# Attention and FP4 feed-forward on one core: the second score pass moved ahead of the small TensorE jobs, the exponential ahead of its step's ScalarE jobs

## The chip, the core and the metric

The kernel runs on one core of a Trainium2 chip. TensorE multiplies, VectorE and ScalarE read its results out of PSUM, GpSimd works on data in SBUF, and SyncE issues the DMAs. Each engine takes its instructions in the order in which they are written and waits on semaphores. The metric is device microseconds for one execution; a row that carries "PE" is TensorE, "DVE" VectorE, "ACT" ScalarE, "POOL" GpSimd, "SP" SyncE.

## The reference

Input is x of shape 4 x 1024 x 128. One layer of attention with 16 heads over a latent of width 64, a layer norm, a feed-forward network whose operands are rounded to FP4 in blocks of 16, and another layer norm.

```python
k_eff = (W_dq.T @ W_uq.T @ W_uk).reshape(nh, hs, n_kvl)
v_eff = transpose((W_uv.T @ W_o.T).reshape(n_kvl, nh, hs), (1, 0, 2))
c_kv = x @ W_dkv.T
q = (x @ W_dq.T @ W_uq.T).reshape(B, T, nh, hs)
q_lat = einsum('bqhd,hdl->bhql', q, k_eff)
attn = softmax(where(causal, einsum('bhql,bkl->bhqk', q_lat, c_kv) / sqrt(hs), -inf))
y = einsum('bhql,hld->bqhd', einsum('bhqk,bkl->bhql', attn, c_kv), v_eff)
x = layernorm(x + y)
gate, up = fp4(x) @ fp4(w_gate).T, fp4(x) @ fp4(w_up).T
x = layernorm(x + fp4(silu(gate) * up) @ fp4(w_down).T)
```

## The kernel before

A batch of 1024 rows is attended in four quads of four heads. A quad is 18 **steps**, so a batch has 72; steps are numbered n = 0 to 71 in a batch, and s = n mod 18 in a quad. The scores are computed twice. The **first pass** (`score_max`, lines 520 and 507) makes rows of scores only so that VectorE can take their row maxima (line 837, `maximum`). The maxima are split in three bf16 parts on GpSimd (`top_split`), transposed (job `mt`), copied by ScalarE (line 686) and written by six small DMAs as extra rows of the query operand. The **second pass** (`score_probs`, lines 537 and 507) then makes transposed scores with the maximum already subtracted, and ScalarE takes their exponential (line 715, `exps`). The **weighing** (`weigh`, line 556) multiplies the values by them into `yt_ps`; it has twelve parts a quad, at steps s = 3, 5, 6, 7, 9, 10, 12, 14, 16, 17 and, in the next quad, 0 and 1. The first pass runs 24 steps ahead of the second.

Both passes write to one ring of three PSUM tiles of two banks. At step n the first pass may start when the exponential of step n-2 has been read out of its tile, and the second pass when the maximum of the first pass of step n-1 has. So the order in the ring is first pass, second pass, first pass, and so on.

Everything else that TensorE does is a **job** (`misc_job`), and nearly all jobs use one PSUM bank, `misc`: a job waits until the reader of the job before has emptied it (`frees`). A table (`jobs`) gives the step of each. `xt`, `k`, `q`, `v` prepare the next batch (steps 6, 7, 12, 15, 18, 19, 24, 25); `yn` (s = 3 and 9) normalizes the attention's output; `mt` (s = 13) is told above; `x1t`, `gate`, `up`, `ht`, `down` are the feed-forward network of the batch before, in eight tiles, `gate` at n = 4 + 6t, `up` at 5 + 6t, `ht` at 20 + 6t, `down` at 42, 43, 64 and 65. ScalarE reads `xt`, `k`, `q`, `v`, `mt`, `x1t`, `gate` and `ht` (`misc_read`); VectorE reads `yn` and `up` and adds `down`, and it makes the rest of `q`. Two steps after `gate` ScalarE also does `sigmoid` (lines 722 and 724), which waits for GpSimd's clamp (line 1151) of what the exponential of `gate` wrote.

The order of each engine is written out by a loop over batches and steps; there is no scheduler. In one step TensorE does: first pass, jobs, second pass, weighing. ScalarE does: reads of the jobs, `first_k_part` (steps 16, 17), `sigmoid`, exponential, copy of `yt_ps`. VectorE does: maximum, then its part of the jobs, then stages of the norms and of the quantization. SyncE's list after step 24 is long: when the last part of `q` is made it issues 24 copies to scratch in DRAM, then four reads, then the six rows of maxima for the quad that starts at step 36. A last loop (b = B) has only the feed-forward network of the last batch.

Of the kernel before, what the change touches and what calls it, by code (L numbers as in the profile page):

```python
# [49 lines left out]
def build(nc, x, w_dq, w_uq, w_dkv, w_uk, w_uv, w_o, w_gate, w_up, w_down, out):  # L50
    B, T, C = x.shape
# [78 lines left out]
    def jobs_at(b, n):  # L130
        return [(kind, b + d, k) for s, kind, d, k in (jobs if b < B else tail) if s == n and 0 <= b + d < B]
# [16 lines left out]
    with ExitStack() as ctx:  # L148
# [171 lines left out]
        def tile_pos(b, a, s):  # L320

            u = a + s // STEPS
            return b + u // QUADS, u % QUADS, s % STEPS
# [93 lines left out]
        def _(pe):  # L417
# [174 lines left out]
            for b in range(B + 1):  # L592
                if b == B:

                    pe.wait_ge(t_exp.sem, t_exp.at(B - 1, BODY - 1))
                for n in range(BODY):
                    if b < B:
                        a, s = n // STEPS, n % STEPS
                        nb, na, ns = tile_pos(b, a, s + STEPS + LEAD)
                        if nb < B:  # L600
                            if n < 2 and b == 0:
                                pe.wait_ge(s_max.sem, STEPS + LEAD)
                            else:
                                pn = b * BODY + n - 2
                                pe.wait_ge(t_exp.sem, pn + 1)
                            score_max(nb, na, ns, 2 * n % 3)
                    for job in jobs_at(b, n):
                        misc_job(*job)
                    if b < B:

                        if nb < B:
                            pe.wait_ge(s_max.sem, b * BODY + n + STEPS + LEAD)
                        else:
                            pe.wait_ge(s_max.sem, B * BODY)
                            pe.wait_ge(t_exp.sem, b * BODY + n - 2)
                        score_probs(b, a, s, (2 * n + 1) % 3)

                    for w, at in enumerate(W_STEP):
                        g = n - at
                        if g % STEPS == 0 and g >= 0 and b < B:  # L620
                            weigh(b, g // STEPS, w)
                        elif g % STEPS == 0 and g < 0 and b > 0:
                            weigh(b - 1, QUADS - 1, w)
# [3 lines left out]
        def _(act):  # L627
# [23 lines left out]

            def misc_read(kind, b, k):
                _, to = bank(kind, b, k)
                if kind == "xt":
                    act.wait_ge(xt_mm.sem, xt_mm.at(b, k))
# [116 lines left out]
            for b in range(B + 1):  # L772
                for n in range(BODY):
                    a, s = n // STEPS, n % STEPS
                    for job in jobs_at(b, n):
                        misc_read(*job)
                    if n in K_PART_AT and b + 1 < B:
                        first_k_part(b + 1, K_PART_AT.index(n))
                    if b > 0:
                        for stage, t in tile_at(b, n, H_A if b < B else TAIL_H_A):  # L780
                            sigmoid(b - 1, t)
                    if b < B:
                        exps(b, a, s)

                    if s == 7 and b < B:
                        out_copy(b, NC * a)
                    if s == 1:
                        if a > 0 and b < B:
                            out_copy(b, NC * a - 1)
                        elif a == 0 and b > 0:  # L790
                            out_copy(b - 1, QUADS * NC - 1)
# [428 lines left out]
```

## Time and profile before

| | us |
|---|---|
| median of 3 runs | 754.0 |
| lowest and highest | 752.06, 757.2 |
| profiled execution, its own time | 758.44 |
| its span | 756.6 |

The span has a stretch of preparation up to the first exponential at 71.7 us, the four batches up to about 665 us, and the tail of the last feed-forward network. In the stretch from 371 to 533 us, which is about one batch, TensorE is busy 136.09 us of 162, VectorE 131.71, ScalarE 101.46, GpSimd 74.91, at a granted TensorE clock of 0.95. Where a view says "idle before" it is the time in which the engine stood still ahead of that group, and the arrow names what ended the wait. A wait for a semaphore shows only with the one that came last.

### The profile page before, as it was taken

The page shows a single profiled execution, that of the slowest core. Times are in us where ns is not written, and L with a number is a line of the kernel's source. Part 1 is how long each engine was busy: PE and PEld are TensorE (multiplying, and loading weights), DVE is VectorE, ACT ScalarE, POOL GpSimd, SP SyncE. Part 2 cuts the span into 40 slices and gives each one's busy share as a digit, 9 for nine tenths or more (in the row PEclk, how much of TensorE's full clock was granted, in tenths as well). Part 3 has the DMA queues.
Part 4 walks back from the last instruction along what each step waited for, and adds up shares of the span by engine and source line. Part 5 has one row for each costly group of instructions (what it writes and reads, how often), then busy time and mean ns, then how long its engine had stood idle before and what let it go on. Part 6 is the DMA issues. An engine that isn't in the chain of part 4 may idle for free.

```text
span 756.6 us, 15168 instructions
## 1 busy us (share of the span) xinstructions
PE 563.6 (74%) x5863; PEld 254.3 (34%) x5863; DVE 532.3 (70%) x981; ACT 412.3 (54%) x598; POOL 316.0 (42%) x441
## 2 busy tenths in 40 slices
PE   4275988589787888788888889696978897862623
PEld 2132333233333434333333334242323342421412
DVE  0389787388889767788788778888787784264461
ACT  2311766377665766565576666564656675742220
POOL 4520032000436654433337464533273536258682
PEclk9655999799998999999898999998899998995565
DMA  3393006602300192020300480203000000000000
GB/s 101 77 241 101 2 3 151 145 2 51 94 5 12 31 210 56 15 52 16 92 16 2 90 196 11 56 10 78 3 16 3 3 2 16 1 15 0 0 14 15
DMA packets 34222, 37.91 MB, mean 50 GB/s; under 512 B 6390, under 2 KB 19766, under 8 KB 34150
## 3 DMA queue, kind: packets, MB, share of 16 engines
q1 hardware_dynamic: 33238, 36.39, 20.0%
q8 instruction: 47, 0.77, 0.4%
q10 hardware_dynamic: 912, 0.54, 0.3%
q14 instruction: 25, 0.20, 0.1%
HBM read 19.64 MB, written 16.78 MB: 48 GB/s over the span
## 4 chain that ended last, share of the span: by engine, by line
PE 39%; DVE 31%; POOL 13%; issue 10%; ACT 4%; DMA 2%; SPq 1%; POOLq 0%; DVEq 0%; ACTq 0%
DVE top L837 19%; PE yt_ps L556 11%; PE ring L537 6%; PE ring L520 5%; PE misc L495 3%; PE ring L507 2%; PE misc L466 2%; POOL eg L1151 2%; POOL hx L1123 2%; POOL hx L1121 2%; POOL hx L1125 1%; DVE z L906 1%; PE misc L455 1%; PE misc L486 1%; DVE hc L963 1%
## 5 line engine op out<-in xcount | busy, mean ns | idle before, releaser
L837 DVE TENSOR_REDUCE top<-ring 128x2 f32<-128x1024 f32 (+3 forms) x384 | 349.6, 948 | 113.4 <-PE ring L507 80.2
L715 ACT ACTIVATE probs<-ring 128x1024 f32<-128x1024 f32 x288 | 293.8, 1027 | 132.1 <-PE ring L507 79.7
L556 PE MATMUL yt_ps<-probs,v_op 128*32 128x512 f32 (+3 forms) x1536 | 171.6, 520 | 0.5 <-ACT probs L715 0.5
L537 PE MATMUL ring<-q_op,k_op 59*128 59x512 bf16 (+3 forms) x768 | 124.0, 346 | 50.2 <-DVE top L837 40.3
L520 PE MATMUL ring<-k_op,q_op 56*128 56x512 f16 (+3 forms) x768 | 127.8, 355 | 44.5 <-ACT probs L715 18.9
L520 PEld LDWEIGHTS ring<-k_op,q_op 56*128 56x128 bf16 x768 | 38.4, 96 | 171.0 <-issue 116.8
L1144 POOL TENSOR_TENSOR r<-r,yq 128x128 f32<-128x128 f32 x32 | 14.6, 457 | 168.3 <-DVE yq L876 168.3
L537 PEld LDWEIGHTS ring<-q_op,k_op 59*128 59x128 f16 x768 | 37.7, 95 | 120.8 <-DVE top L837 58.7
L507 PE MATMUL ring<-ident,mask_s 64*128 64x64 bf16 x1024 | 59.5, 198 | 0.0
L507 PEld LDWEIGHTS ring<-ident,mask_s 64*128 64x128 bf16 x1024 | 47.7, 102 | 17.7 <-issue 5.0
L507 PEld LDWEIGHTS ring<-ident,mask_t 64*128 64x128 bf16 x1024 | 47.2, 100 | 18.2 <-issue 6.8
L507 PE MATMUL ring<-ident,mask_t 64*128 64x64 bf16 x1024 | 52.0, 196 | 0.0
L1151 POOL TENSOR_SCALAR eg<-eg 128x352 f32<-128x352 f32 x32 | 35.1, 1098 | 28.0 <-ACT eg L698 27.6
L722 ACT ACTIVATE eg<-eg,one 128x352 f32<-128x352 f32 x32 | 18.7, 586 | 41.0 <-POOL eg L1151 41.0
L556 PEld LDWEIGHTS yt_ps<-probs,v_op 128*32 128x32 f32 x1536 | 30.9, 110 | 29.6 <-issue 18.5
L1121 POOL TENSOR_TENSOR hx<-hx,hc 128x352 f32<-128x352 f32 x32 | 29.8, 931 | 20.7 <-DVE hc L966 20.7
L486 PE MATMUL ring<-ident,hx 128*128 128x128 f32 (+1 forms) x24 | 6.7, 414 | 42.6 <-POOL hx L1125 42.6
L1080 POOL TENSOR_SCALAR top_parts<-top_all 128x32 bf16<-128x32 f32 x16 | 4.8, 297 | 68.3 <-DVE top_all L846 68.2
L1123 POOL TENSOR_TENSOR hx<-hx,hc 128x352 f32<-128x352 f32 x32 | 29.8, 930 | 2.5
L1155 POOL TENSOR_TENSOR h<-gu,eg 128x352 f32<-128x352 f32 x32 | 29.8, 930 | 0.0
L963 DVE TENSOR_SCALAR hc<-hx 128x352 uint32<-128x352 uint32 x32 | 15.8, 492 | 16.3 <-POOL hx L1160 16.3
L1125 POOL TENSOR_TENSOR hx<-hx,h_sc 128x352 f32<-128x352 f32 x32 | 25.2, 787 | 2.5
(170 smaller groups left out, 758.4 us busy)
## 6 DMA issues: line engine op xcount, KB each, us to landing
q_op<-scratch_q SPq DMA_DIRECT2D x32, 224.0 KB
k_op<-scratch_k SPq DMA_DIRECT2D x32, 224.0 KB
scratch_k<-k_part SPq DMA_DIRECT2D x32, 192.0 KB, 3.3
scratch_q<-q_part SPq DMA_DIRECT2D x32, 128.0 KB, 3.1
scratch_q<-q_part SPq DMA_DIRECT2D x16, 192.0 KB, 3.3
xp<-in_L_attn_x_dram SPq DMA_DIRECT2D x4, 512.0 KB, 4.4
r<-in_L_attn_x_dram SPq DMA_DIRECT2D x8, 256.0 KB, 2.8
out_dram<-z SPq DMA_DIRECT2D x8, 256.0 KB, 2.3
```

Of the source, the lines that this page charges most:

```text
L507: last = nc.tensor.matmul(ring[slot][:, e, at + HALF * half:at + HALF * (half + 1)], mask[group, half, :], ident16[group, group], start=Fa ...
L520: last = nc.tensor.matmul(ring[slot][:, e, at:at + n], q_op[lo:lo + ROWS, pair, i * P:(i + 1) * P], k_op[lo:lo + ROWS, pair, kc * CHUNK:kc ...
L537: last = nc.tensor.matmul(ring[slot][:, e, at:at + n], k_op[lo:lo + rows, pair, j * P:(j + 1) * P], q_op[lo:lo + rows, pair, (c + 1) * CHU ...
L556: last = nc.tensor.matmul(yt_ps[32 * q:32 * (q + 1), lo:CHUNK], v_op[:, j, 4 * a + q, :], probs[:, (STEPS * a + tile) % P_RING, q % 2, at: ...
L715: nc.scalar.activation(probs[:, n % P_RING, :, :], ring[(2 * n + 1) % 3][:, :, :], ACT.Exp, scale=SCALE).then_inc(t_exp.sem, 1)
L837: last = nc.vector.tensor_reduce(top[:, kc, :, p, i], ring[slot][:, :, at:at + n], AX.X, ALU.max)
L963: nc.vector.tensor_scalar(hc[:, n, :, :].bitcast(U32), hx[:, n, :, :].bitcast(U32), 0x7F800000, None, ALU.bitwise_and).then_inc(he_v.sem, 1)
L1121: nc.gpsimd.tensor_tensor(dst, dst, magic, ALU.add).then_inc(s1.sem, 1)
L1123: nc.gpsimd.tensor_tensor(dst, dst, magic, ALU.subtract).then_inc(s2.sem, 1)
L1125: nc.gpsimd.tensor_tensor(dst, dst, sc_, ALU.mult).then_inc(s3.sem, 1)
L1151: nc.gpsimd.tensor_scalar(eg[:, n, :], eg[:, n, :], EXP_TOP, None, ALU.min).then_inc(e_p.sem, 1)
L1155: nc.gpsimd.tensor_tensor(hn.rearrange("p n k -> p (n k)"), gu[:, n, :], eg[:, n, :], ALU.mult).then_inc(h_p.sem, 1)
```

## The change

On TensorE the second score pass of a step directly follows the first, and the jobs come behind both, ahead of the weighing as before. On ScalarE the exponential of a step comes ahead of that step's job reads, `first_k_part` and `sigmoid`; the copy of `yt_ps` stays where it is. No instruction is added or taken away, and VectorE, GpSimd and SyncE keep their lists.

```diff
--- before.py
+++ after.py
@@ -604,8 +604,6 @@
                                 pn = b * BODY + n - 2
                                 pe.wait_ge(t_exp.sem, pn + 1)
                             score_max(nb, na, ns, 2 * n % 3)
-                    for job in jobs_at(b, n):
-                        misc_job(*job)
                     if b < B:
 
                         if nb < B:
@@ -614,7 +612,8 @@
                             pe.wait_ge(s_max.sem, B * BODY)
                             pe.wait_ge(t_exp.sem, b * BODY + n - 2)
                         score_probs(b, a, s, (2 * n + 1) % 3)
-
+                    for job in jobs_at(b, n):
+                        misc_job(*job)
                     for w, at in enumerate(W_STEP):
                         g = n - at
                         if g % STEPS == 0 and g >= 0 and b < B:
@@ -772,6 +771,8 @@
             for b in range(B + 1):
                 for n in range(BODY):
                     a, s = n // STEPS, n % STEPS
+                    if b < B:
+                        exps(b, a, s)
                     for job in jobs_at(b, n):
                         misc_read(*job)
                     if n in K_PART_AT and b + 1 < B:
@@ -779,9 +780,6 @@
                     if b > 0:
                         for stage, t in tile_at(b, n, H_A if b < B else TAIL_H_A):
                             sigmoid(b - 1, t)
-                    if b < B:
-                        exps(b, a, s)
-
                     if s == 7 and b < B:
                         out_copy(b, NC * a)
                     if s == 1:
```

TensorE, batch 1, steps 40 and 41 (`L520` and `L507` with mask_s the first pass, `L537` the second, `L480` the jobs `gate` and `up`, `L556` the weighing), before:

```order
L520 MATMUL ring<-k_op,q_op 128x256 [waits t_exp]
L520 MATMUL ring<-k_op,q_op 128x256
L507 MATMUL ring<-ident,mask_s 128x64 x4
L520 MATMUL ring<-k_op,q_op 128x256 x2
L507 MATMUL ring<-ident,mask_s 128x64 x4
L480 MATMUL misc<-wu_t,xq_t 128x352 [waits x1t_cp,g_cp]
L537 MATMUL ring<-q_op,k_op 128x512 [waits s_max]
L537 MATMUL ring<-q_op,k_op 128x512
L556 MATMUL yt_ps<-probs,v_op 32x384 [waits t_exp]
```

and now:

```order
L520 MATMUL ring<-k_op,q_op 128x256 [waits t_exp]
L520 MATMUL ring<-k_op,q_op 128x256
L507 MATMUL ring<-ident,mask_s 128x64 x4
L520 MATMUL ring<-k_op,q_op 128x256 x2
L507 MATMUL ring<-ident,mask_s 128x64 x4
L537 MATMUL ring<-q_op,k_op 128x512 [waits s_max]
L537 MATMUL ring<-q_op,k_op 128x512
L480 MATMUL misc<-wu_t,xq_t 128x352 [waits x1t_cp,g_cp]
L556 MATMUL yt_ps<-probs,v_op 32x384 [waits t_exp]
```

The job `up` stood between the two passes and now stands between the second pass and the weighing; its waits are the same.

ScalarE, batch 1, steps 29 to 31 (`L715` the exponential, `L722` and `L724` `sigmoid` of step 30, `L686` the read of the job `mt` of step 31), before:

```order
L699 COPY gs<-misc 128x352
L715 ACTIVATE probs<-ring 128x1024 [waits av_mm,t_mm] x2
L722 ACTIVATE eg<-eg,one 128x352 [waits h_clamp]
L724 ACTIVATE eg<-eg 128x352 [waits h_ln]
L715 ACTIVATE probs<-ring 128x1024 [waits av_mm,t_mm]
L686 COPY top_t<-misc 96x128 [waits mrow_in,mt_mm]
L715 ACTIVATE probs<-ring 128x1024 [waits av_mm,t_mm]
```

and now (line numbers are one less there):

```order
L714 ACTIVATE probs<-ring 128x1024 [waits av_mm,t_mm]
L697 ACTIVATE eg<-misc 128x352 [waits g_gu,h_h,g_mm]
L698 COPY gs<-misc 128x352
L714 ACTIVATE probs<-ring 128x1024 [waits av_mm,t_mm] x2
L721 ACTIVATE eg<-eg,one 128x352 [waits h_clamp]
L723 ACTIVATE eg<-eg 128x352 [waits h_ln]
L714 ACTIVATE probs<-ring 128x1024 [waits av_mm,t_mm]
L685 COPY top_t<-misc 96x128 [waits mrow_in,mt_mm]
```

The rows read alike in sequence, but each exponential between two jobs is now the one of the earlier job's own step: the one ahead of `gate`'s read is that of step 28, the two behind it are steps 29 and 30, so `sigmoid` stands behind the exponential of its step and no longer in front of it.

## Rows read from the trace of the kernel before

**Rows 1.** The page: span, busy time by engine, shares of the chain that ended last.

```profile
span 756.6 us, 15168 instructions
...
PE 563.6 (74%) x5863; PEld 254.3 (34%) x5863; DVE 532.3 (70%) x981; ACT 412.3 (54%) x598; POOL 316.0 (42%) x441
...
PE 39%; DVE 31%; POOL 13%; issue 10%; ACT 4%; DMA 2%; SPq 1%; POOLq 0%; DVEq 0%; ACTq 0%
```

**Rows 2.** Groups by line; columns: count, busy us, mean ns, idle before, its releasers.

```profile
L837 DVE TENSOR_REDUCE top<-ring 128x2 f32<-128x1024 f32 (+3 forms) x384 | 349.6, 948 | 113.4 <-PE ring L507 80.2 <-PE ring L520 31.7
L715 ACT ACTIVATE probs<-ring 128x1024 f32<-128x1024 f32 x288 | 293.8, 1027 | 132.1 <-PE ring L507 79.7 <-PE ring L537 49.7
...
L520 PE MATMUL ring<-k_op,q_op 56*128 56x512 f16 (+3 forms) x768 | 127.8, 355 | 44.5 <-ACT probs L715 18.9 <-DMA k_op<-scratch_k 17.9 <-DVE top L837 7.2
L537 PE MATMUL ring<-q_op,k_op 59*128 59x512 bf16 (+3 forms) x768 | 124.0, 346 | 50.2 <-DVE top L837 40.3 <-issue 9.3
...
L722 ACT ACTIVATE eg<-eg,one 128x352 f32<-128x352 f32 x32 | 18.7, 586 | 41.0 <-POOL eg L1151 41.0
```

**Rows 3.** The same view: ScalarE's two copies that empty `misc` after `ht`.

```profile
L704 ACT COPY h_t<-misc 128x256 f32<-128x256 f32 x24 | 9.2, 384 | 3.6 <-PE misc L486 3.6
...
L705 ACT COPY h_t<-misc 96x128 f32<-96x128 f32 x24 | 6.6, 275 | 0.0
```

**Rows 4.** Timeline (start, length, instruction, idle before), batch 0, step 12.

```profile
89.06 1.23 DVE L837 TENSOR_REDUCE top<-ring 128x2 f32<-128x1024 f32 x1 [0.31 <-PE ring L507]
...
89.45 1.12 PE L451 MATMUL misc<-x_t,bk 128*128 128x512 f32 x2
...
90.50 0.39 PE L537 MATMUL ring<-q_op,k_op 59*128 59x512 bf16 x2
```

**Rows 5.** Timeline, batch 1, steps 40 and 41.

```profile
294.80 0.86 PE L480 MATMUL misc<-wg_t,xq_t 128*128 128x352 f32 x2
294.91 1.29 DVE L837 TENSOR_REDUCE top<-ring 128x2 f32<-128x256 f32 x2 [0.76 <-PE ring L507]
...
295.59 0.28 PE L537 MATMUL ring<-q_op,k_op 59*128 59x256 bf16 x2
...
295.69 0.46 ACT L698 ACTIVATE eg<-misc 128x352 f32<-128x352 f32 x1 [1.20 <-PE misc L480]
...
296.05 0.45 ACT L699 COPY gs<-misc 128x352 f32<-128x352 f32 x1
...
296.55 0.86 PE L480 MATMUL misc<-wu_t,xq_t 128*128 128x352 f32 x2
...
297.66 0.85 PE L556 MATMUL yt_ps<-probs,v_op 128*32 128x384 f32 x8
```

**Rows 6.** Timeline, batch 1, steps 48 to 50.

```profile
315.37 1.09 POOL L1151 TENSOR_SCALAR eg<-eg 128x352 f32<-128x352 f32 x1
...
316.50 0.59 ACT L722 ACTIVATE eg<-eg,one 128x352 f32<-128x352 f32 x1 [3.10 <-POOL eg L1151]
...
317.52 1.01 ACT L715 ACTIVATE probs<-ring 128x1024 f32<-128x1024 f32 x1
...
318.44 0.79 POOL L1125 TENSOR_TENSOR hx<-hx,h_sc 128x352 f32<-128x352 f32 x1
...
318.58 0.28 PE L520 MATMUL ring<-k_op,q_op 56*128 56x256 f16 x2 [2.41 <-ACT probs L715]
```

**Rows 7.** Timeline of SyncE's DMA issues, batch 1.

```profile
261.31 1.26 SPq L353 DMA_DIRECT2D scratch_k<-k_part  x3
...
280.62 4.29 SPq L371 DMA_DIRECT2D q_op<-top_t  x6
```

**Rows 8.** Timeline of TensorE, batch 1, step 36.

```profile
287.25 0.39 PE L537 MATMUL ring<-q_op,k_op 59*128 59x512 bf16 x2 [2.64 <-DVE top L837]
```

**Rows 9.** Timeline, batch 1, step 24, the job `q`.

```profile
256.73 1.13 PE L451 MATMUL misc<-x_t,aq 128*128 128x512 f32 x2 [0.36 <-DVE gu L939]
...
257.89 0.69 ACT L672 ACTIVATE q_part<-misc,q_scale 128x512 bf16<-128x512 f32 x1 [1.57 <-PE misc L451]
```

## The prediction, made before the changed kernel ran

> **What bounds the kernel now.** I read the page first, then the groups by line, then timelines of single steps. The profiled execution took 758.44 us (span 756.6 [rows 1]); the median of three runs is 754.0, so the profile lies 4.4 us above it. Sums are made against 758.44 and then moved down by 4.4.
>
> The page gives no single bound. TensorE is busy 74% of the span, VectorE 70%, ScalarE 54%, and the chain that ended last alternates: TensorE 39%, VectorE 31%, waits that nothing explains 10% [rows 1]. The groups by line say how [rows 2]: VectorE stood idle 113.4 us ahead of the maxima, always for a first pass; ScalarE 132.1 us ahead of the exponentials, always for a second pass; TensorE 44.5 us ahead of the first pass and 50.2 us ahead of the second. Of the 44.5, 17.9 us are one DMA in the preparation and 18.9 us waits for an exponential. Of the 50.2, 40.3 us are waits for a maximum. So TensorE is the engine on which the others mostly wait, and what the change does to the time is read from TensorE's order: does it stand idle more or less.
>
> **What the second pass wins by going first.** It starts earlier by the length of the job, and so does the exponential. Who waits for an exponential? ScalarE itself was idle 132.1 us ahead of it, so ScalarE gains nothing. TensorE waited 18.9 us for one before a first pass. That is the whole prize, and its largest pieces have one cause. At step 48 [rows 6] ScalarE's `sigmoid` stands ahead of the exponential. It waits for GpSimd's clamp, which ends at 315.37 + 1.09 = 316.46; then come `sigmoid`'s two halves, then the exponential from 317.52 to 318.53, and the first pass of step 50 starts at 318.58 after 2.41 us of idle. Six waits of this kind are 2.41 us each, 14.5 of the 18.9. With the exponential in front, the first pass of step 50 needs not wait for the clamp. But the next thing is late already: the job `ht` of step 50 needs GpSimd's product, which ends at 318.44 + 0.79 = 319.23, and the weighing of step 50 stands behind `ht` in both kernels. So only what had stood behind the stall and now runs inside it is won, the second pass of step 50 with its handover and part of the wait behind `ht`: about 0.7 us of 2.41. Two of the six lie in a stretch that a DMA chain bounds (below) and win nothing. Four times 0.7 is 2.8; of the other 4.4 us I take half, since behind them VectorE is as late as ScalarE: **minus 5 us**.
>
> It also runs in front of jobs that themselves wait for `misc` to be emptied, so 0.32 us of each such wait is used. But where ScalarE is in the chain of such a job (`q`, then `v`), its read now comes later by as much. I take ten places where it isn't, at 0.15: **minus 1.5 us**.
>
> **What it costs: cover.** The second pass waits for the maximum of the first pass of the step before. Till now a job ran in that time. Once the trace shows it whole [rows 4]: the maximum ends at 89.06 + 1.23 = 90.29; the job `k` runs from 89.45 to 90.5; the second pass starts at 90.50, 0.2 after the maximum, with no idle ahead of it. Now TensorE stands idle from 89.45 to 90.5, runs the second pass, and then the job: the weighing behind comes 1.0 us later. This is the upper price. Where the maximum has ended before the first pass is out, the price is zero. In batch 0, with no feed-forward jobs to slow TensorE down, the maxima are late at nearly every step; there are eight such jobs outside the stretch of the DMA chain (`yn` at n = 9, 21, 39, 45, 57, 63; `k` at 12; `q` at 18). One at 1.0 and seven at 0.45, the middle: **plus 4 us**. In batches 1 to 3 TensorE arrives later at most steps; I allow one full and two half cases in three batches: **plus 2 us**.
>
> **What it costs: the one bank of the jobs.** ScalarE now reads a job behind its step's exponential, and the next job waits for that read. The pair `gate`, `up` at a step with no weighing between them [rows 5]. Before: `gate` at 294.80, read from 295.69 to 296.05 + 0.45 = 296.50, `up` at 296.55, so the bank is free just in time. Now: second pass at 294.80, `gate` at 295.15 (the pass keeps TensorE for about 0.35 of its 0.39 us [rows 4], an estimate), the exponential from 295.3 to 296.3 (1027 ns [rows 2]), the read to 297.2. TensorE has meanwhile done the first pass of step 41 (until 296.55), the second, which needs the maximum ended at 294.91 + 1.29 = 296.20, and stands at `up` from 296.9 to 297.25. The weighing then starts at 298.03 and not at 297.66: 0.37 us. Steps 4, 22 and 40 of three batches have no weighing: 9 x 0.4, **plus 3.6 us**. At the other `gate`s a weighing of about 1 us hides it.
>
> The pair `ht`, `yn` is of the same kind. A second pass at time 0, exponential from 0.4 to 1.45, two copies of 0.38 and 0.28 us [rows 3]: `misc` is free at 2.1. TensorE is at `yn` at about 1.7, after its own pass, `ht`, a first pass and a second that waits a little for its maximum (four groups of 0.35 to 0.5 us, an estimate from rows 4 and 5). 0.3 us at five pairs a batch, three batches: **plus 4.5 us**.
>
> **What it costs: the chain through SyncE.** The last part of `q` (job of step 24, 256.73 [rows 9]) is read by ScalarE at 257.89, worked on by VectorE and GpSimd, and SyncE starts its list at 261.31; the six rows of maxima are issued from 280.62 to 284.9 [rows 7], and the second pass of step 36 starts at 287.25 after 2.64 us of idle [rows 8]. The view names VectorE for it, but the rows land just then. So in batches 0 to 2 whatever steps 25 to 35 win or lose is swallowed, and the start of the list moves with the job of step 24. There the second pass now comes first (0.32 us), and the read waits for the exponential that the second pass started (0.4 + 1.02 against 0.32 + 1.13, even): 0.4 us in three batches, **plus 1.2 us**. SyncE's other transfers wait for nothing that moves by more than 1 us, and they have many us of slack.
>
> **Costed at nothing.** VectorE takes the product of `up` 0.3 us later at its source, hidden by the 1.23 us maximum ahead of it in VectorE's queue; gone, it would be 24 x 0.3 = 7 us, my bound for this. `sigmoid` comes one exponential (1.03 us) later, and ScalarE waited 41.0 us for the clamp ahead of it [rows 2], so it mostly takes the place of waiting; GpSimd's product of it is due three steps later. The tail has no exponential and no scores, and its order is the same.
>
> **Sum.** 4 + 2 + 3.6 + 4.5 + 1.2 - 5 - 1.5 = 8.8, so about 9 us slower: 767 for an execution like the profiled one, **763 us** against the median of 754. Bounds: every cover term at its upper end and no prize gives 8 + 4 + 3.6 + 7 + 1.2 + 7 = 31 slower; every cover term at zero and the prize whole gives 18.9 + 3 less, 22 faster. Each end needs all terms at once.
>
> **A rule of the notes against the row.** The Trainium skill, "Perfetto Trace Analysis", section Identifying the Most-Contended Engine, says that the engine of highest occupancy is the one to work on. By that rule this change, which takes no work from TensorE, would leave the time alone: 754. The trace shows three engines near each other and none near full [rows 1], and a second pass whose free cover order alone makes [rows 4]; so here I go by order. The rule's result is the second case below.
>
> **The rivals, with chances.**
> - *Forecast, slower by 8 to 18 us, 0.50.* As above.
> - *Nothing measurable, 0.35.* The waits are elastic: a TensorE that arrives later at one second pass finds its maximum ready at the next, as VectorE with 70% is nearly as full, and the stalls behind `sigmoid` [rows 6] and SyncE's chain [rows 7] swallow what the steps in front of them lost. For it: after each such stall the account begins at zero. Against it: VectorE was itself idle 113.4 us for TensorE, so a late first pass mostly costs. If half of the positive terms (15.3) is swallowed, it is 7.6 - 6.5, plus 1: 755 us.
> - *Faster, 0.12.* The exponential is the real clock of the ring: with it early, the six stalls of 2.41 us go whole, the small ones too (18.9), and the cover terms fall to half (8). 754 - 11 = 743. Its place is the first pass behind `sigmoid`; it decides if the first pass of step 50 lets VectorE and through it GpSimd run ahead far enough that `ht` is no longer late by the time TensorE is there, more than about 1.5 us won per stall. Against it: `ht`'s product comes out of GpSimd's own queue behind the clamp.
> - *Slower by over 20 us, 0.03.* More idle ahead of second passes takes TensorE's clock down to 1.2 GHz for the steps behind; a `k` of 1.12 us would be 2 us. The mean clock of 0.95 would show it. 780 us.
>
> A measurement of this kernel can tell about 1%, 7.5 us. Slower by more: 0.50 + 0.03, less 0.03 for the low edge of the forecast's case, 0.50. Within: 0.35 + 0.03 - 0.01 for the low edge of that case, 0.37. Faster: 0.12 + 0.01 = 0.13. The range reaches from 748, leaving out most of the faster case, to 776, leaving out the last one and the top of the forecast.
>
> **What would show it.** Right: TensorE's idle ahead of `L537` for a maximum up from 40.3 to 55 us or more; idle ahead of `up` and `yn` for ScalarE's copies, 5 to 9 us more; idle ahead of the first pass for an exponential down from 18.9 to under 8; ScalarE's wait for the clamp down from 41.0 by 10 or more; the second passes of step 36 in batches 0 to 2 still idle ahead. Wrong: if the wait for the exponential falls and VectorE's idle ahead of the maxima falls below 105 us, the ring gained and the faster case holds; if TensorE's idle sums move from one line to another and their total stays within 3 us, the second case holds.

## The result, and the profile after

The changed kernel takes 762.5 us, the median of 20 runs (756.9 to 766.9); the kernel before took 755.1 beside it (20 runs, 752.1 to 760.8). The ratio is 1.0084, with a 95% interval of 1.0059 to 1.0109: 7.3 us slower by the medians, 6.3 by the ratio (0.0084 x 755). The forecast was 763. Below, microseconds of an experiment are worked out from its ratio in the same way. Ratios and mean clocks leave out executions in a slower state of the chip, such as one of experiment 11 with 863.1 us at a mean granted clock of 0.557.

The page of the changed kernel, its rows for the span, the busy time of each engine and the chain that ended last:

```profile
span 756.9 us, 15168 instructions
...
PE 559.1 (74%) x5863; PEld 250.3 (33%) x5863; DVE 533.2 (70%) x981; ACT 411.7 (54%) x598; POOL 315.2 (42%) x441
...
PE 40%; DVE 29%; POOL 12%; issue 10%; ACT 6%; DMA 2%; SPq 1%; POOLq 0%; ACTq 0%; DVEq 0%
```

The span is that of before, 756.9 against 756.6 us [rows 1], though the medians lie 7.3 us apart. Each of the two traces is one execution, and they are unlike in their clock: the one of after (own time 758.84 us, 3.6 below its median) had a mean granted clock of 0.892, the one of before (758.44, 3.3 above its median) 0.876. At the higher clock TensorE was busy 4.5 us less with the same 5863 instructions. So the traces are read here for idle time and for what ended it. Added up over the timeline from the first exponential to the last, TensorE's idle is 100.7 us before and 105.5 after: 4.8 more.

Groups by line of the changed kernel (count, then busy time and mean ns, then the idle before them with what ended it):

```profile
L835 DVE TENSOR_REDUCE top<-ring 128x2 f32<-128x1024 f32 (+3 forms) x384 | 349.4, 948 | 103.6 <-PE ring L507 62.5 <-PE ring L520 39.5
...
L520 PE MATMUL ring<-k_op,q_op 56*128 56x512 f16 (+3 forms) x768 | 128.3, 357 | 25.4 <-DMA k_op<-scratch_k 17.1 <-DVE top L835 7.2 <-ACT probs L714 0.7
L537 PE MATMUL ring<-q_op,k_op 59*128 59x512 bf16 (+3 forms) x768 | 122.3, 341 | 75.1 <-DVE top L835 62.6 <-issue 10.5
...
L466 PE MATMUL misc<-ident,yt 128*128 128x128 f32 x128 | 21.4, 291 | 6.8 <-ACT h_t L704 6.2
L480 PE MATMUL misc<-wu_t,xq_t 128*128 128x352 f32 x48 | 20.6, 511 | 3.3 <-ACT gs L698 3.3
...
L721 ACT ACTIVATE eg<-eg,one 128x352 f32<-128x352 f32 x32 | 18.7, 586 | 33.6 <-POOL eg L1149 33.6
...
L486 PE MATMUL misc<-ident,hx 128*128 128x128 f32 (+1 forms) x72 | 13.7, 302 | 14.2 <-POOL hx L1123 14.1
...
L870 DVE RECIPROCAL inv<-misc 128x16 f32<-128x16 f32 x32 | 8.2, 257 | 22.4 <-PE misc L466 21.9
```

The same view of before, for four small groups that are not among the rows ahead of the prediction:

```profile
L466 PE MATMUL misc<-ident,yt 128*128 128x128 f32 x128 | 21.6, 293 | 4.8 <-ACT h_t L705 2.7 <-ACT yt L731 1.1
...
L480 PE MATMUL misc<-wu_t,xq_t 128*128 128x352 f32 x48 | 20.6, 511 | 0.9
...
L486 PE MATMUL misc<-ident,hx 128*128 128x128 f32 (+1 forms) x72 | 14.0, 307 | 4.6 <-POOL hx L1125 4.6
...
L872 DVE RECIPROCAL inv<-misc 128x16 f32<-128x16 f32 x32 | 8.0, 249 | 17.4 <-PE misc L466 17.4
```

Read in pairs. Ahead of the second pass (`L537`) TensorE's wait for a maximum rose from 40.3 to 62.6 us [rows 2]. Ahead of the first pass (`L520`) its wait for an exponential fell from 18.9 to 0.7. Ahead of `yn` (`L466`) and `up` the waits for ScalarE's copies rose from 2.7 to 6.2 and from nothing that is listed (0.9 in all) to 3.3. Ahead of `ht` (`L486`) the wait for GpSimd's product rose from 4.6 to 14.1. ScalarE waited less for the clamp (`L721`), 33.6 against 41.0, and VectorE less ahead of the maxima, 103.6 against 113.4 [rows 2]. But VectorE's wait for `yn` (`L870`, before `L872`) rose from 17.4 to 22.4: part of its idle only changed its place.

Timeline of the changed kernel (start, length, instruction, idle before), batch 0, step 12, against [rows 4]:

```profile
88.81 0.38 PE L520 MATMUL ring<-k_op,q_op 56*128 56x512 f16 x2
...
90.08 0.39 PE L537 MATMUL ring<-q_op,k_op 59*128 59x512 bf16 x2 [0.83 <-DVE top L835]
...
90.40 1.13 PE L451 MATMUL misc<-x_t,bk 128*128 128x512 f32 x2
...
91.46 1.07 PE L556 MATMUL yt_ps<-probs,v_op 128*32 128x512 f32 x8
```

The cover is gone, as predicted: TensorE is idle for 0.83 us where `k` had run, and `k` and the weighing (`L556`) come behind. From the start of the first pass to the weighing it is 91.46 - 88.81 = 2.65 us. Before it was 1.74, with the weighing at 90.82 in the same view: 0.91 more.

Timeline, batch 1, steps 40 and 41, the pair `gate` (first row) and `up` (last), against [rows 5]:

```profile
296.66 0.86 PE L480 MATMUL misc<-wg_t,xq_t 128*128 128x352 f32 x2
296.77 1.02 ACT L714 ACTIVATE probs<-ring 128x1024 f32<-128x1024 f32 x1 [1.61 <-PE ring L507]
...
298.04 0.46 ACT L698 COPY gs<-misc 128x352 f32<-128x352 f32 x1
...
298.55 0.86 PE L480 MATMUL misc<-wu_t,xq_t 128*128 128x352 f32 x2 [0.36 <-ACT gs L698]
```

The exponential (`L714`) runs ahead of the reads of `gate`, the second read ends at 298.50, and `up` stands idle until then: 0.36 us. The sum had 0.35.

Timeline, batch 1, steps 48 to 50, against [rows 6]:

```profile
316.46 1.09 POOL L1149 TENSOR_SCALAR eg<-eg 128x352 f32<-128x352 f32 x1
...
317.58 0.59 ACT L721 ACTIVATE eg<-eg,one 128x352 f32<-128x352 f32 x1 [1.60 <-POOL eg L1149]
...
319.53 0.79 POOL L1123 TENSOR_TENSOR hx<-hx,h_sc 128x352 f32<-128x352 f32 x1
...
320.46 0.52 PE L486 MATMUL misc<-ident,hx 128*128 128x128 f32 x3 [2.05 <-POOL hx L1123]
...
320.91 1.91 PE L556 MATMUL yt_ps<-probs,v_op 128*32 128x512 f32 x8
```

The clamp (`L1149`) still ends late, at 317.55, and `sigmoid` (`L721`) waits for it, but the first pass does not: its 2.41 us [rows 6] are gone. In its place `ht` of step 50 (`L486`) stands idle for 2.05 us, until GpSimd's product (`L1123`) ends at 320.32. The weighing behind it takes 1.91 us, where the same eight products take 1.07 in the timeline of step 12. The view by windows of the changed kernel shows the clock beside it (stretch, its length, busy time of TensorE's matmuls and weight loads, VectorE, ScalarE and GpSimd, then the granted clock):

```profile
320.90:322.80 1.90, 1.90 (x11) 0.23 (x12) 0.00 (x0) 0.53 (x2) 1.05 (x2) 0.52 0.04 7
```

The granted clock is 0.52, about the lower of TensorE's two levels (1.2 of 2.4 GHz), behind 2.05 us of standing still. The kernel before has the same: 1.93 us for the weighing of step 50, behind its 2.41 us.

### The profile page after: what moved, and what is told of

The parts are those of the page before. It is cut to its first block, busy times and chain, and to the rows that moved or that the text cites. A ratio compares the mean times of both kernels' runs of the same rounds, so it can differ in the third digit from the quotient of the medians.

```text
span 756.9 us, 15168 instructions
## 1 busy us (share of the span) xinstructions
PE 559.1 (74%) x5863; PEld 250.3 (33%) x5863; DVE 533.2 (70%) x981; ACT 411.7 (54%) x598; POOL 315.2 (42%) x441
## 3 DMA queue, kind: packets, MB, share of 16 engines
q1 hardware_dynamic: 33238, 36.39, 19.9%
## 4 chain that ended last, share of the span: by engine, by line
PE 40%; DVE 29%; POOL 12%; issue 10%; ACT 6%; DMA 2%; SPq 1%; POOLq 0%; ACTq 0%; DVEq 0%
DVE top L835 19%; PE yt_ps L556 13%; PE ring L520 5%; PE ring L537 5%; PE misc L495 3%; PE misc L466 2%; PE misc L480 2%; POOL eg L1149 2%; PE ring L507 2%; ACT probs L714 2%; POOL hx L1121 2%; POOL hx L1119 2%; POOL hx L1123 1%; DVE z L904 1%; PE misc L451 1%
## 5 line engine op out<-in xcount | busy, mean ns | idle before, releaser
L835 DVE TENSOR_REDUCE top<-ring 128x2 f32<-128x1024 f32 (+3 forms) x384 | 349.4, 948 | 103.6 <-PE ring L507 62.5
L714 ACT ACTIVATE probs<-ring 128x1024 f32<-128x1024 f32 x288 | 294.3, 1027 | 193.5 <-PE ring L507 123.5
L537 PE MATMUL ring<-q_op,k_op 59*128 59x512 bf16 (+3 forms) x768 | 122.3, 341 | 75.1 <-DVE top L835 62.6
L556 PE MATMUL yt_ps<-probs,v_op 128*32 128x512 f32 (+3 forms) x1536 | 172.9, 524 | 0.6 <-ACT probs L714 0.5
L520 PE MATMUL ring<-k_op,q_op 56*128 56x512 f16 (+3 forms) x768 | 128.3, 357 | 25.4 <-DMA k_op<-scratch_k 17.1
L520 PEld LDWEIGHTS ring<-k_op,q_op 56*128 56x128 bf16 x768 | 38.2, 96 | 165.1 <-issue 103.9
L537 PEld LDWEIGHTS ring<-q_op,k_op 59*128 59x128 f16 x768 | 37.8, 95 | 114.5 <-DVE top L835 90.4
L507 PE MATMUL ring<-ident,mask_s 64*128 64x64 bf16 x1024 | 58.8, 197 | 0.0
L507 PEld LDWEIGHTS ring<-ident,mask_t 64*128 64x128 bf16 x1024 | 47.2, 100 | 19.2 <-issue 6.2
L507 PEld LDWEIGHTS ring<-ident,mask_s 64*128 64x128 bf16 x1024 | 47.0, 100 | 15.7 <-issue 3.8
L507 PE MATMUL ring<-ident,mask_t 64*128 64x64 bf16 x1024 | 51.8, 196 | 0.0
L1149 POOL TENSOR_SCALAR eg<-eg 128x352 f32<-128x352 f32 x32 | 35.0, 1094 | 35.0 <-ACT eg L697 34.6
L556 PEld LDWEIGHTS yt_ps<-probs,v_op 128*32 128x32 f32 x1536 | 30.8, 110 | 47.1 <-issue 34.7
L486 PE MATMUL ring<-ident,hx 128*128 128x128 f32 (+1 forms) x24 | 6.7, 414 | 42.9 <-POOL hx L1123 42.9
L721 ACT ACTIVATE eg<-eg,one 128x352 f32<-128x352 f32 x32 | 18.7, 586 | 33.6 <-POOL eg L1149 33.6
L466 PE MATMUL misc<-ident,yt 128*128 128x128 f32 x128 | 21.4, 291 | 6.8 <-ACT h_t L704 6.2
```

What stands on the lines that cost most here:

```text
L466: last = nc.tensor.transpose(to[:, n * P:(n + 1) * P], yt[:, k % 2, n * P:(n + 1) * P], ident[:, :])
L507: last = nc.tensor.matmul(ring[slot][:, e, at + HALF * half:at + HALF * (half + 1)], mask[group, half, :], ident16[group, group], start=Fa ...
L520: last = nc.tensor.matmul(ring[slot][:, e, at:at + n], q_op[lo:lo + ROWS, pair, i * P:(i + 1) * P], k_op[lo:lo + ROWS, pair, kc * CHUNK:kc ...
L537: last = nc.tensor.matmul(ring[slot][:, e, at:at + n], k_op[lo:lo + rows, pair, j * P:(j + 1) * P], q_op[lo:lo + rows, pair, (c + 1) * CHU ...
L556: last = nc.tensor.matmul(yt_ps[32 * q:32 * (q + 1), lo:CHUNK], v_op[:, j, 4 * a + q, :], probs[:, (STEPS * a + tile) % P_RING, q % 2, at: ...
L714: nc.scalar.activation(probs[:, n % P_RING, :, :], ring[(2 * n + 1) % 3][:, :, :], ACT.Exp, scale=SCALE).then_inc(t_exp.sem, 1)
```

## The experiments

All are the kernel before with an edit, or the changed kernel with one; the ratio is always to the kernel before. In the diffs `first` is the condition for the new order in a step.

**1. TensorE's part alone, ScalarE's as before.**

```diff
-                    for job in jobs_at(b, n):
-                        misc_job(*job)
...
                         score_probs(b, a, s, (2 * n + 1) % 3)
+                    for job in jobs_at(b, n):
+                        misc_job(*job)
```

> Only TensorE's part of the change: the second score pass ahead of the jobs; ScalarE keeps the old order. Theory A (TensorE loses its cover: it stands idle for maxima where a job used to run): most of the loss of the whole change stays, +5 to +9 us (ratio 1.007 to 1.012), idle ahead of L537 for a maximum stays near 63 us. Rival B (the loss is that ScalarE reads the jobs later, so the bank misc comes free later): +0 to +2 us, since the reads again come first. Idle ahead of the first pass for an exponential comes back to 10 to 19 us in both.

760.0 us, ratio 1.0061 [1.0023, 1.0099]. Groups by line:

```profile
L520 PE MATMUL ring<-k_op,q_op 56*128 56x512 f16 (+3 forms) x768 | 127.1, 353 | 48.1 <-ACT probs L719 22.5 <-DMA k_op<-scratch_k 17.9 <-DVE top L847 7.2
L537 PE MATMUL ring<-q_op,k_op 59*128 59x512 bf16 (+3 forms) x768 | 121.3, 338 | 73.7 <-DVE top L847 62.4 <-issue 9.5
...
L466 PE MATMUL misc<-ident,yt 128*128 128x128 f32 x128 | 21.4, 291 | 1.2 <-ACT h_t L709 1.2
```

TensorE's part alone gives 4.6 us of loss, anywhere from 1.7 to 7.5 by the interval, and the whole of the wait for maxima (62.4 us against 62.6). With it the prize is not there: the first pass still waits 22.5 us for exponentials. The bank's price is there in small part: `yn` waits 1.2 us for ScalarE and `up` 2.1, in place of 6.2 and 3.3.

**2. ScalarE's part alone, TensorE's as before.**

```diff
+                    if b < B:
+                        exps(b, a, s)
                     for job in jobs_at(b, n):
                         misc_read(*job)
...
-                    if b < B:
-                        exps(b, a, s)
```

> Only ScalarE's part of the change: the exponential ahead of the reads, first_k_part and sigmoid; TensorE keeps the old order (jobs, then second pass). Theory A: the reads come a whole exponential later, and only then the next job can run, but second passes keep their cover: between -2 and +4 us. Rival B: +6 to +12 us, since here ScalarE must even wait for the second pass before it reads a job that was done ahead of it.

809.2 us, ratio 1.0713 [1.0662, 1.0763]: far beyond every theory. Two groups by line, and a timeline of batch 1, steps 15 and 16 (`L719` is the exponential here, `L669` ScalarE's read of a `k`, `L480` the job `gate`):

```profile
L466 PE MATMUL misc<-ident,yt 128*128 128x128 f32 x128 | 21.3, 291 | 29.0 <-ACT h_t L709 24.5 <-ACT yt L735 4.4
L480 PE MATMUL misc<-wu_t,xq_t 128*128 128x352 f32 x48 | 20.6, 511 | 20.2 <-ACT gs L703 20.2
```

```profile
242.46 1.02 ACT L719 ACTIVATE probs<-ring 128x1024 f32<-128x1024 f32 x1 [1.80 <-PE ring L507]
...
243.38 0.58 ACT L669 COPY kf<-misc 128x512 f32<-128x512 f32 x1
...
244.01 0.86 PE L480 MATMUL misc<-wg_t,xq_t 128*128 128x352 f32 x2 [1.38 <-ACT kf L669]
...
244.81 0.34 PE L537 MATMUL ring<-q_op,k_op 59*128 59x384 bf16 x2
...
245.36 1.02 ACT L719 ACTIVATE probs<-ring 128x1024 f32<-128x1024 f32 x1 [1.40 <-PE ring L507]
```

The order makes a ring of waits. The read of `k` stands behind the exponential of step 15 (242.46 to 243.48); `gate` waits 1.38 us for the read; in TensorE's old order the second pass stands behind `gate`, so it starts at 244.81; and the exponential of step 16, with ScalarE idle 1.40 us, waits for it. `yn` and `up` together wait 44.7 us for ScalarE (24.5 and 20.2). TensorE's idle is 142.7 us against 100.7. So the two halves of the change do not add: ScalarE's costs 54 us alone. Behind TensorE's new order, where a second pass no longer waits for what a job waits for, it costs 1.7 us (1.0084 - 1.0061), and the overlapping intervals do not tell that from zero.

**3. The whole change, but only at steps 0 to 23 of batches 1 to 3.** In the traces this stretch had looked quicker.

```diff
-                    first = True
+                    first = b > 0 and n < 24
```

> The whole change, but only at steps n < 24 of batches 1 to 3; the old order in batch 0 and from step 24 on. In the profile of the changed kernel the exponentials of steps 0 to 24 span 53.7, 54.4 and 48.0 us in batches 1 to 3 against 57.6, 59.2 and 51.8 before, and the steps from 24 on span 2 to 9 us more. Theory C (the change wins at the steps whose jobs wait for VectorE, and loses at the others): -6 to -12 us, ratio 0.984 to 0.992. Rival D (the steps after 24 only give back a lead that something else bounds, the chain through SyncE or GpSimd, whatever their order is): -3 to +2 us.

754.9 us, ratio 0.9994 [0.9962, 1.0025]. No gain. The stretch had been measured between starts of exponentials, and these now stand at another place of their step. From here on stretches go by the start of the weighing, which both orders have last.

**4. The old order, with `sigmoid` alone behind the exponential of its step.**

```diff
+                    if b < B:
+                        exps(b, a, s)
                     if b > 0:
                         for stage, t in tile_at(b, n, H_A if b < B else TAIL_H_A):
                             sigmoid(b - 1, t)
-                    if b < B:
-                        exps(b, a, s)
```

> TensorE in the old order; ScalarE in the old order but for sigmoid, which comes behind the exponential of its step (the reads of the jobs stay ahead of it). It takes away what I named as the cause of the six 2.41 us waits of the first pass for an exponential. Theory A: these go, what is won is what the job ht does not take back, -2 to -6 us (ratio 0.992 to 0.997). Rival: the clamp and the product of GpSimd bound these steps, 0 +- 1 us. Idle of the first pass for an exponential under 6 us in both.

755.2 us, ratio 1.0005 [0.9969, 1.0041]. Groups by line:

```profile
L520 PE MATMUL ring<-k_op,q_op 56*128 56x512 f16 (+3 forms) x768 | 128.7, 358 | 28.4 <-DMA k_op<-scratch_k 18.0 <-DVE top L847 7.0 <-ACT probs L719 2.7
...
L486 PE MATMUL misc<-ident,hx 128*128 128x128 f32 (+1 forms) x72 | 14.4, 313 | 17.5 <-POOL hx L1135 17.5
```

The wait for the exponential is gone, 2.7 us against 18.9. `ht` waits 17.5 us for GpSimd against 4.6. TensorE's idle fell by 2.8 us in all (97.9 against 100.7), and of the time nothing is seen: by the interval between 2.3 us won and 3.1 lost. In TensorE's old order the prize is worth nothing that the runs can tell: it is one wait in two places.

**5 and 6. The whole change in batch 0 alone, and in batches 1 to 3 alone.**

```diff
-                    first = True
+                    first = b == 0
```

and `b > 0` in the second.

> The whole change, but only in batch 0. Theory A (lost cover at steps whose maximum is late): by the start times of the weighings, batch 0 has 3 to 4 us more in the changed kernel and in the one with TensorE's part alone, at steps 3 to 18, 24 to 46 and 50 to 63, so +3 to +5 us here (ratio 1.004 to 1.007). Rival D (the whole is elastic: what batch 0 loses is got back later): 0 +- 1 us.

> The whole change, but only from batch 1 on (batch 0 in the old order). Theory A as predicted: the bank of the jobs and the chain through SyncE cost about 9 us, cover 2, against a prize of 6, so +3 to +5 us. Rival E (in batches 1 to 3 wins and losses cancel, and all the loss is batch 0's): -1 to +1.5 us.

Batch 0 alone 757.1 us, 1.0024 [0.9994, 1.0055]; the others alone 759.6, 1.0047 [1.0019, 1.0075]. That is +1.8 and +3.6 us, together 5.4 of the 6.3; only the second is clear of zero. The wait for maxima rose by 2.3 us in the first (42.6) and 19.9 in the second (60.2). Between the weighings of step 3 of batch 0 and step 0 of batch 1 the traces show 126.0 us before, 129.7 after and 131.2 in batch 0 alone, so the traces say about +4 or +5 where the runs say +1.8, with an interval from -0.5 to +4.2. Whether batch 0 costs 2 or 4 us stays open.

**7. The whole change, but ScalarE reads `gate` and `ht` ahead of the exponential as before.**

```diff
+                    early = lambda job: job[0] in ("gate", "ht")
+                    for job in jobs_at(b, n):
+                        if early(job):
+                            misc_read(*job)
                     if b < B:
                         exps(b, a, s)
                     for job in jobs_at(b, n):
-                        misc_read(*job)
+                        if not early(job):
+                            misc_read(*job)
```

> The whole change, but ScalarE reads the jobs gate and ht ahead of the exponential of their step again (the other reads, first_k_part and sigmoid stay behind it). It takes away what I priced as the one bank of the jobs, 8.1 us. Theory A: idle ahead of up and yn for ScalarE's copies falls from 9.5 to under 4 us and the time by 3 to 8 us against the changed kernel, 754 to 760 us. Rival F (that wait only takes the place of a wait for a maximum at the same step): idle ahead of the second passes grows by as much, time 760 to 763 us.

758.1 us, ratio 1.0029 [1.0001, 1.0057], against 1.0084 for the whole change: about 4 us won, and the two intervals stand apart, by a hair. Groups by line:

```profile
L537 PE MATMUL ring<-q_op,k_op 59*128 59x512 bf16 (+3 forms) x768 | 123.3, 343 | 76.1 <-DVE top L852 63.8 <-issue 10.6
...
L466 PE MATMUL misc<-ident,yt 128*128 128x128 f32 x128 | 21.7, 294 | 1.2 <-ACT h_t L709 1.2
...
L480 PE MATMUL misc<-wu_t,xq_t 128*128 128x352 f32 x48 | 20.6, 511 | 2.1 <-ACT gs L703 2.1
```

The two waits for ScalarE are down to 1.2 and 2.1 us, while the wait for a maximum is 63.8, 1.2 higher. So the bank's price was real, and was partly handed on. The same two waits stand in experiment 1. Between it and this one the exponential moves ahead of `sigmoid` and the other reads: the first pass waits 0.7 us for exponentials instead of 22.5, and the ratios, 1.0061 and 1.0029, lie 2.4 us apart with intervals that overlap.

**8. Experiment 4, and `ht` of tiles 2 and 5 (steps 32 and 50) one step later.**

```diff
-        jobs += [(4 + 6 * t, "gate", -1, t), (5 + 6 * t, "up", -1, t), (20 + 6 * t, "ht", -1, t)]
+        jobs += [(4 + 6 * t, "gate", -1, t), (5 + 6 * t, "up", -1, t), (20 + 6 * t + (t in (2, 5)), "ht", -1, t)]
```

> TensorE and ScalarE in the old order, sigmoid behind its exponential as in e4_sigmoid, and the job ht of tiles 2 and 5 (steps 32 and 50) one step later. In e4_sigmoid the waits for an exponential went from 19.1 to 2.8 us of idle and those of ht for GpSimd rose from 4.6 to 17.5, with no change in the time. If ht is what holds the steps then, idle ahead of ht falls under 8 us and the time by 3 to 8 us against the kernel before (ratio 0.990 to 0.996). Rival G (GpSimd's chain bounds the stretch whatever stands where): 0 +- 1.5 us, and the idle turns up ahead of another line.

747.6 us, ratio 0.9902 [0.9874, 0.9931]: quicker than both kernels. Groups by line, then the timeline of batch 1 from the second pass of step 50 on:

```profile
L520 PE MATMUL ring<-k_op,q_op 56*128 56x512 f16 (+3 forms) x768 | 126.5, 352 | 29.9 <-DMA k_op<-scratch_k 17.6 <-DVE top L847 7.2 <-ACT probs L719 4.8
L537 PE MATMUL ring<-q_op,k_op 59*128 59x512 bf16 (+3 forms) x768 | 121.4, 340 | 60.7 <-DVE top L847 43.1 <-issue 16.7
...
L486 PE MATMUL misc<-ident,hx 128*128 128x128 f32 (+1 forms) x72 | 14.0, 306 | 3.3 <-POOL hx L1135 3.3
```

```profile
314.95 0.39 PE L537 MATMUL ring<-q_op,k_op 59*128 59x512 bf16 x2 [0.36 <-DVE top L847]
...
315.33 1.07 PE L556 MATMUL yt_ps<-probs,v_op 128*32 128x512 f32 x8
...
316.82 0.39 PE L520 MATMUL ring<-k_op,q_op 56*128 56x512 f16 x2 [0.42 <-ACT probs L719]
...
317.46 0.52 PE L486 MATMUL misc<-ident,hx 128*128 128x128 f32 x3 [0.25 <-POOL hx L1135]
```

The first pass of step 51 waits 0.42 us and `ht`, now in the same step, 0.25. The weighing of step 50 takes 1.07 us. From the weighing of step 48 to that of step 50 it is 3.5 us, where it was 7.1 before, 6.1 in the changed kernel and 7.1 in experiment 4. That `ht` has left this stretch is not the reason: to the weighing of step 52 it is 7.1 us, against 11.1 before and 11.4 in experiment 4.

Part of the gain goes with TensorE's clock. The view by windows, the kernel before and then this one:

```profile
318.90:326.00 7.10, 6.06 (x63) 2.09 (x59) 4.17 (x6) 4.31 (x6) 1.96 (x3) 0.76 0.03 6
```

```profile
314.00:321.00 7.00, 5.97 (x91) 2.65 (x89) 5.59 (x10) 5.70 (x10) 4.79 (x6) 1.00 0.03 6
```

In about the same busy time (6.06 and 5.97 us) TensorE does 63 matmuls at a granted clock of 0.76, and 91 at 1.00. Either edit alone leaves a long stand here: 2.41 us ahead of the first pass in experiment 10, 2.86 ahead of `ht` in experiment 4, where the eight products behind it again take 1.93 us. From the first exponential to the last, the trace of experiment 8 is 13.1 us shorter than that of before: 4.7 of it is idle of TensorE (96.0), 8.4 is busy time with the same instructions. These are single executions, whose own times lie 12.5 us apart. How much of the 7.4 us that the ratio gives is idle and how much is clock, no run separates.

Not every place pays, either. The stall of step 32 lies ahead of SyncE's chain, which ends at step 36. In batches 1 and 2 the weighings of steps 30 and 34 came closer together (9.6 and 11.1 us, now 8.0 each), but those of steps 23 and 36 did not (32.4 and 31.6 us, now 31.9 and 32.0): the second pass of step 36 stands idle 3.7 and 3.8 us, before 2.6 and 0.3. In batch 3, which prepares no batch and has no such chain, steps 23 to 36 went from 29.3 to 26.2.

**9 and 10. The same edit of `ht` on the whole change, and on the kernel before with nothing else.** The diff is the one of experiment 8.

> The whole change, and ht of tiles 2 and 5 one step later (steps 33 and 51). Theory H (the change is a loss of cover and of the bank, and the wait of ht for GpSimd is a separate thing that both orders share): it wins as much on the changed kernel as e8_ht did on e4_sigmoid, 6 to 9 us, so 753 to 757 us, -0.4 to +0.3% against the kernel before. Rival: with the second pass first there is nothing left behind ht but the weighing, so less is won, 0 to 3 us, 759 to 762 us.

> The kernel before with ht of tiles 2 and 5 one step later and nothing else; sigmoid stays ahead of its exponential. Theory H (two waits stand in a row, for the exponential behind sigmoid and for ht behind GpSimd, and each alone hides the other): -1 to +1 us, and the first pass still waits 15 to 20 us for exponentials. Rival: ht was the whole of it, -5 to -8 us as in e8_ht.

On the whole change 752.0 us, 0.9950 [0.9914, 0.9985], 10 us under the changed kernel (1.0084 - 0.9950, times 755). Alone 757.3 us, 1.0001 [0.9962, 1.0041], with these groups by line:

```profile
L520 PE MATMUL ring<-k_op,q_op 56*128 56x512 f16 (+3 forms) x768 | 128.6, 357 | 45.1 <-ACT probs L719 19.1 <-DMA k_op<-scratch_k 18.2 <-DVE top L847 7.2
...
L486 PE MATMUL misc<-ident,hx 128*128 128x128 f32 (+1 forms) x72 | 15.6, 333 | 0.2 <-POOL hx L1135 0.2
```

The mirror of experiment 4: now `ht` waits 0.2 us and the first pass its old 19.1. Either edit alone gives nothing, 1.0005 and 1.0001; both give 0.9902. And 0.9950 against 0.9902 is the price of the rest of the changed order once this stall is gone: 3.6 us, by intervals that just overlap.

**11. Experiment 8, and on TensorE the second pass first at the steps of `k`, `q` and `v` in batches 1 to 3.**

```diff
-                    first = False
+                    first = b > 0 and any(j[0] in ("q", "k", "v") for j in jobs_at(b, n))
```

> e8_ht, and in batches 1 to 3 the second pass first at the steps whose jobs are k, q or v (12, 15, 18, 19, 24, 25). There the job itself waits for VectorE (7.7 + 2.7 us of idle in the kernel before). If the wait for the product of up and the wait for the maximum end one behind the other on VectorE, as in the changed kernel, the second pass only takes over the idle time: -1.5 to +1.5 us against e8_ht. If the order was what held it, -3 to -6 us against e8_ht.

749.2 us, ratio 0.9920 [0.9890, 0.9949], no better than 0.9902. Groups by line:

```profile
L537 PE MATMUL ring<-q_op,k_op 59*128 59x512 bf16 (+3 forms) x768 | 123.2, 344 | 68.1 <-DVE top L847 48.3 <-issue 19.1
...
L451 PE MATMUL misc<-x_t,aq 128*128 128x512 f32 x12 | 7.7, 727 | 0.1
```

The job `q` does not wait any more (0.1 us against 6.5), and the second pass waits 48.3 us for a maximum against 43.1. The wait was mostly handed on.

## Why the prediction was right, and where its terms were not

The forecast holds in sign, size and kind: 8.8 us predicted, 7.3 measured by the medians and 6.3 by the ratio, from the two costs that it named: lost cover (4.6 us in experiment 1) and the reads of the one bank (4.1 won back in experiment 7). The two shares overlap, and their intervals are too wide to say which is the larger. It is not right term by term. That the sum came out so near is in part luck: the bank was priced at about twice what it cost, and of the prize set against it nothing was to be seen.

- **The cover (+4 and +2).** Right. The place that the trace had shown whole cost 0.91 us against 1.0. TensorE's wait for maxima rose by 22.3 us, over the 15 that were asked for, and experiment 1, which has this term alone, costs 4.6 us by its ratio (interval 1.7 to 7.5). The 22.3 us of wait cost so little because most of it took the place of other waits: TensorE's whole idle rose by 4.8, and in experiment 1 by 8.0 (100.7 to 108.7) with its 62.4 us for maxima.
- **The split by batches.** The sum by batches was 4 for batch 0; the runs give 1.8, with an interval that includes 4. Not settled.
- **The one bank of the jobs (+3.6 and +4.5).** Right in mechanism, too large. One wait at `up` was 0.36 us against 0.35. All waits for ScalarE's copies together rose by 5.7 us (`yn` 3.8 to 6.2, `up` from nothing listed to 3.3), inside the 5 to 9 that were named; but experiment 7, which takes the reads back, wins about 4 us and not 8.1. The waits were smaller than the 24 that were priced, and not all of them is loss: of the 6.2 us that experiment 7 takes away (`yn` 5.0, `up` 1.2), 1.2 came back as wait for a maximum.
- **The prize (-5).** Not borne out, and the step of it that failed is "what had stood behind the stall and now runs inside it is won". Experiment 4 collects 16.2 of the 18.9 us of waiting, in TensorE's old order, and the time stays at 1.0005. The pieces moved inside the stall were not on its path: it ends when `ht` of step 50 gets GpSimd's product, in either order, and only with `ht` itself out of the way (experiment 8) is the early exponential worth something. From the weighing of step 48 to that of step 50 the changed kernel won 1.0 us in batch 1 (7.1 to 6.1), but experiment 4, which has the same early exponential, none. Over all six places (steps 30 to 32 and 48 to 50 of batches 1 to 3) it is 40.2 us before and 37.1 after, but two steps further on nothing is left of it: to the weighings of steps 34 and 52, 62.8 and 63.1. The count was off as well: the trace of before has five waits of 2.41 us, not six, so 12.1 of the 18.9; at step 50 of batch 3 no first pass is left to wait, and `ht` itself stands 3.20 us for GpSimd. That two of the places lie ahead of SyncE's chain and win nothing was right (experiment 8).
- **Waits of jobs covered (-1.5).** Not separated. The job `q` waited 6.5 us before and 0.0 after, and experiment 11 suggests that such a wait is only handed to the second pass.
- **SyncE's chain (+1.2).** Unsettled, with one sign failed. Job `q` of step 24 and the start of SyncE's list, then TensorE at step 36, of the changed kernel, batch 1, against [rows 7 to 9]:

```profile
259.04 1.12 PE L451 MATMUL misc<-x_t,aq 128*128 128x512 f32 x2
...
263.75 0.31 SPq L353 DMA_DIRECT2D scratch_k<-k_part  x1
```

```profile
289.00 0.38 PE L537 MATMUL ring<-q_op,k_op 59*128 59x512 bf16 x2
```

From `q` to the list it is 4.71 us, before 261.31 - 256.73 = 4.58: 0.13 later and not 0.4. And the second pass of step 36 has no idle ahead of it, where "still idle" was said; that would fit steps before it that have become as slow as the chain. It is idle in batch 0 (9.2 us) and batch 2 (1.3); before it was 9.0, 2.6 and 0.3 in batches 0 to 2.
- **The wait for the clamp.** It fell by 7.4 us, not by 10 or more. In experiment 4, where `sigmoid` alone moves, it fell by 12.8 (28.2). TensorE's new order works against it: in experiment 1, where `sigmoid` stays in front, the wait rose by 8.0 (49.0).
- **The rivals.** The sign that was given for the faster case came out in full, a wait for the exponential near zero and VectorE's idle ahead of maxima below 105 us (103.6), and the kernel was slower. It was a bad sign: against those 9.8 us VectorE's wait ahead of `L870`, for `yn`, grew by 5.0. An idle sum of one group says nothing unless the others are added. The total of TensorE's idle, the sign for "nothing measurable", did tell: +4.8, beyond the 3 us. The fourth case, a lower clock, did not come: from 371 to 533 us the granted clock is 0.94 against 0.95, and over the whole span 0.892 against 0.876. The rule of the Trainium skill, "Perfetto Trace Analysis", section Identifying the Most-Contended Engine, as the prediction applied it, would have given 754. TensorE, the engine of highest occupancy (74%), kept its 5863 instructions, and orders of the same work took 747.6 to 809.2 us. So on this kernel the measurement decides against that reading of the rule: order alone moved the time.

## What to carry to other kernels

Before an instruction is moved up because someone waits for it, look for the next wait of the same engine a step further on: two waits in a row that end within a microsecond of each other are one cost, and only moving both wins (0 and 0 apart, 1.0% together). Such a stand can cost more than its own length: behind it eight products of TensorE took 1.93 us, and 1.07 where it was gone. A job between two dependent passes is free cover; put behind them it costs its length where the pass must wait, but only a part of the listed waits reaches the end. And where jobs share a buffer, the order of the engine that fills it and that of the engine that empties it must be looked at as a pair: the emptying half alone cost 7%, the filling half alone 0.6%, both 0.8%.

## What the chip showed that was not expected

Among executions of one kernel the slower ones mostly have the lower mean granted clock of TensorE. The 20 runs of the changed kernel go from 756.9 us (span 754.8) at 0.897 to 766.9 (span 765.1) at 0.881, with a correlation of -0.8 and about 3 us per 0.01 of clock; the 12 of experiment 8 have -0.9 and 5 us. It is not so tight everywhere: experiments 3 to 7 have -0.5 to -0.6, and the 26 executions of the kernel before on the chip of experiments 9 to 11 have -0.3. The mean over a kernel's runs differs with its order too: on that chip it was 0.880 for the kernel before, 0.878 for experiment 10, 0.887 for experiment 11 and 0.896 for experiment 9. In the two high ones the five stands of over 2 us at steps 32 and 50 are gone. But the clock alone does not rank kernels: experiment 9 has the highest and is no quicker than experiment 11. Two single traces can hide 1%, as the two here did. The idle sums were the better guide here (+4.8 us where the ratio says +6.3), though only roughly: in experiment 4 the sum fell by 2.8 with no gain. Whether the clock makes the time here or the waits make the clock, and why one execution of the same code runs at another mean clock, no run here tells.
